# Expert stage of a two-layer graph network: one register load of TensorE moved behind the transposes, and the order of copies, scaling and adds on VectorE and GpSimd changed

## The reference

```
x = x + gnn0(layernorm(x), adj)          # (A @ (x @ W + b)) / column sums of A
x = x + ffn(layernorm(x))                # the expert stage, below
x = x + gnn1(layernorm(x), A)            # relu(D^-1/2 (A + I) D^-1/2 x @ W.T + b)
x = x + bit_operation(layernorm(x))      # adds 0 or 2 to columns 128..159

def ffn(x):                              # 8 experts, two for each row
    scores = softmax(x @ Wg + bg)
    the two best of 8, their scores divided by their sum -> combine[row, expert]
    h = gelu(x @ W1[e] + b1[e])          # 256 -> 1024
    y = h @ W2[e] + b2[e]                # 1024 -> 256
    return sum over e of combine[:, e] * y[e]
```

## Time and profile before

| what | value |
|---|---|
| median of 3 runs | 1072.77 us (1072.39 to 1073.36) |
| profiled execution, its time | 1071.65 us |
| its span in the profile | 1069.8 us |
| TensorE busy | 950.6 us, 89% |
| VectorE busy | 552.7 us, 52% |
| ScalarE busy | 402.5 us, 38% |
| GpSimd busy | 352.5 us, 33% |
| granted TensorE clock, mean over the span | 0.954 |

### The profile page before, as it was taken

How to read it: one execution, slowest core, us unless ns; L and a number is a source line. 1 busy time by engine, 2 the same in 40 slices (tenths; PEclk the granted TensorE clock), 3 DMA queues, 4 the chain that set the end, 5 groups by cost and what they waited for, 6 DMA issues and landing times. The chain is left out here.

```text
span 1069.8 us, 21961 instructions
## 1 busy us (share of the span) xinstructions
PE 950.6 (89%) x6628; PEld 613.0 (57%) x6629; DVE 552.7 (52%) x1631; ACT 402.5 (38%) x820; POOL 352.5 (33%) x414
## 2 busy tenths in 40 slices
PE   4988999999912799999999999999829999999993
PEld 1444544444411688888888888888714454444541
DVE  6744213137598655655556556566536334161654
ACT  4863659676787323232232332323202101010111
POOL 3510000024566234545445445454535320110110
PEclk9999999999965899999999999999969999999997
DMA  9886898899787422222323223233259978876770
GB/s 335 321 302 195 281 328 321 314 337 381 263 266 197 151 40 43 51 45 46 54 40 55 45 45 52 42 50 50 44 154 391 409 275 283 312 239 192 232 266 26
DMA packets 91023, 199.83 MB, mean 187 GB/s; under 512 B 13312, under 2 KB 46848, under 8 KB 90848
## 3 DMA queue, kind: packets, MB, share of 16 engines
q1 hardware_dynamic: 69248, 164.17, 43.8%
q0 software_dynamic: 17552, 30.88, 14.6%
q10 hardware_dynamic: 4176, 4.19, 1.2%
HBM read 176.54 MB, written 22.68 MB: 186 GB/s over the span
## 5 line engine op out<-in xcount | busy, mean ns | idle before, releaser
L956 PE MATMUL bank<-adj_f,feat 128*128 128x512 f16 x1024 | 239.2, 389 | 17.7 <-DMA adj_f<-in_adjT 16.0
L1217 ACT ACTIVATE act_f<-bank,b_sb 128x256 f32<-128x256 f32 x296 | 124.2, 471 | 288.5 <-PE bank L1157 288.5
L1157 PE MATMUL bank<-rT,experts 128*128 128x256 f16 x1776 | 202.3, 274 | 6.1 <-DVE rT L1240 2.2
L1169 PE MATMUL bank<-experts,act_h 128*128 x1776 | 203.1, 275 | 3.5 <-DVE y_f L1255 3.5
L1157 PEld LDWEIGHTS bank<-rT,experts 128*128 x1776 | 169.6, 98 | 38.7 <-issue 16.2
L1169 PEld LDWEIGHTS bank<-experts,act_h 128*128 128x128 f16 x1776 | 173.9, 99 | 24.5 <-issue 3.7
L1590 PE MATMUL bank<-adj_g,feat 128*128 128x512 f16 x768 | 178.5, 386 | 1.0 <-POOL feat L1420 1.0
L956 PEld LDWEIGHTS bank<-adj_f,feat 128*128 128x128 f16 x1024 | 97.2, 96 | 143.5 <-issue 15.3
L840 ACT ACTIVATE spent<-adj_f 128x1024 f16<-128x1024 f32 x128 | 135.1, 1055 | 33.7 <-DMA adj_f<-in_adjT 28.2
L1089 POOL DMA_INDIRECT x_rows<-y,token x74 | 119.2, 1611 | 68.5 <-DVE y L1265 49.0
L1590 PEld LDWEIGHTS bank<-adj_g,feat 128*128 128x128 f16 x768 | 73.6, 96 | 93.9 <-issue 1.5
(11 more groups left out here) (261 smaller groups left out, 889.4 us busy)
## 6 DMA issues: line engine op xcount, KB each, us to landing
adj_f<-in_adjT SPq DMA_DIRECT2D x128, 512.0 KB, 6.7
adj_g<-in_adjT SPq DMA_DIRECT2D x72, 512.0 KB, 6.9
adj_early<-in_adjT SPq DMA_DIRECT2D x24, 512.0 KB, 6.1
adj_g<-in_adjT SPq DMA_DIRECT2D x48, 256.0 KB, 3.1
unit_f<-in_W SPq DMA_DIRECT2D x16, 512.0 KB, 7.4
stage<-in_W SPq DMA_DIRECT2D x12, 512.0 KB, 6.2
x_ring<-in_x POOLq DMA_DIRECT2D x16, 256.0 KB, 6.9
x_rows<-agg SPq DMA_DIRECT2D x4, 1024.0 KB, 8.9
```

The costliest lines, as they stand in the source:

```text
L956: last = pe.matmul(mine(s)[ib * DC + c][:, :], feat0[:, j, h, c * P:(c + 1) * P], adj_0[j % RING][:, ib * HALF_SWEEP:(ib + 1) * HALF_SWEEP ...
L1157: last = pe.matmul(pb[2 + q][:, k * SLOT:(k + 1) * SLOT], w1_part(e * DC + (f // FQ * W2_UNIT0 + c), wh)[:, (f % FQ) * P:(f % FQ + 1) * P] ...
L1169: last = pe.matmul(pb[6 + r][:, 0:D], act_h[:, ah, f, r * P:(r + 1) * P], experts[:, ds(e * DC + (W2_UNIT0 + f // UH), 1), wh, (f % UH) * ...
L1217: last = a.activation(act_f[q][:, k, :], pb[2 + q][:, k * SLOT:(k + 1) * SLOT], ACT.Gelu, bias=b1_sb[:, ds(e * FC + (2 * q + k), 1)], scal ...
```

## The change

Five edits, all in the expert stage:

1. TensorE reads `e2` behind `transposes(s + 2)`, not at the top of the pass.
2. VectorE copies the shares (`gates`) before `rT`.
3. VectorE does `take_y(s)` ahead of the fourth `split_hidden`, not behind it.
4. GpSimd waits for each half of y by itself, add 0 for half 0 and add 1 for half 1, within the loop and after it.
5. `y_free` counts halves: GpSimd gives it after each add has landed (it begins at `SR`), and VectorE waits for it before each half that it scales.

```diff
         @block.gpsimd
-            pool.sem_inc(sem("y_free"), 1)
+            pool.sem_inc(sem("y_free"), SR)
...
-            def scaled(s):
-                pool.wait_ge(sem("y_scaled"), (s + 2) * SR)
+            def scaled(s, r):
+                pool.wait_ge(sem("y_scaled"), (s + 1) * SR + r + 1)
                 pool.sem_inc(sem("waited"), 1)
...
             with pool.Fori(0, last) as s:
-                scaled(s)
+                scaled(s, 0)
                 add_rows(0)
                 rows_free(s + 3)
                 gather(pool, token, AHEAD * SR)
                 landed_until(s, 0)
+                pool.sem_inc(sem("y_free"), 1)
+                scaled(s, 1)
                 add_rows(1)
                 pool.wait_ge(sem("rows_loaded"), (s + 5) * (16 * SR))
                 landed_until(s, 1)
                 pool.sem_inc(sem("y_free"), 1)
                 take_tokens(s + 1)
-            scaled(last)
             for r in range(SR):
+                scaled(last, r)
                 add_rows(r)
                 landed_until(last, r)
...
         @block.tensor
             with pe.Fori(0, last_slot) as s:
                 e = expert_of(s + 1)
-                e2 = expert_of(s)
                 pe.wait_ge(sem("rT_ready"), s + 2)
                 for q in range(FQ):
                     first_layer(s + 1, e, q)
                 transposes(s + 2)
+                e2 = expert_of(s)
                 second_layer_may_begin(s, e2)
...
         @block.vector
             def next_rows(s):
                 v.wait_ge(sem("rT_ps_ready"), s + 1)
-                v.tensor_copy(rT[...], pb[0][...]).then_inc(sem("rT_ready"), 1)
                 v.tensor_copy(gates[...], rows[...]).then_inc(sem("gates_taken"), 1)
+                v.tensor_copy(rT[...], pb[0][...]).then_inc(sem("rT_ready"), 1)
...
             def scale_y(s):
                 v.wait_ge(sem("y_taken"), s + 2)
                 v.wait_ge(sem("gates_taken"), s + 1)
-                v.wait_ge(sem("y_free"), s + 1)
                 for r in range(SR):
+                    v.wait_ge(sem("y_free"), s * SR + r + 1)
                     v.tensor_scalar(y[:, r, :], y_f[:, r, :], gates[...], None, ALU.mult).then_inc(sem("y_scaled"), 1)
...
             with v.Fori(0, last_slot) as s:
                 next_rows(s + 2)
-                for q in range(FQ):
+                for q in range(FQ - 1):
                     split_hidden(s + 1, q)
                 take_y(s)
+                split_hidden(s + 1, FQ - 1)
                 scale_y(s)
```

More of the change, by code:

```diff
@@ L1239, in next_rows @@
                 v.wait_ge(sem("rT_ps_ready"), s + 1)
-                v.tensor_copy(rT[:, :, :, :].rearrange("p h c n -> p (h c n)"), pb[0][:, :].bitcast(F16)).then_inc(sem("rT_ready"), 1)
                 v.tensor_copy(gates[:, ds(s * SR, SR)], rows[:, :, ds(D + e, 1)].rearrange("p r a -> p (r a)")
                               ).then_inc(sem("gates_taken"), 1)
+                v.tensor_copy(rT[:, :, :, :].rearrange("p h c n -> p (h c n)"), pb[0][:, :].bitcast(F16)).then_inc(sem("rT_ready"), 1)
             def split_late(k):
```

## The result

The changed kernel ran 1061.84 us in the median (1059.44 to 1062.92, 4 runs), the kernel before beside it 1072.58 (1071.67 to 1073.36, 4 runs): ratio 0.9897, 95% interval 0.9878 to 0.9916. That is 10.7 us less; forecast were 1063.3 us and a range of 1061 to 1067.5. The profiled execution took 1062.92 us with a span of 1061.1.

The account below looks back on a forecast made before the run. TensorE, busy 89% of the span, was taken as the bound, with a sequencer hole at each loop top. Terms -9.3 + 0.3 - 0.1 - 0.4 = -9.5 us gave 1063.3 us; range for 8 in 10, 1061 to 1067.5.

Parts of the forecast that it names:

- Where the hole is from: Top of the expert loop: TensorE's sequencer needs 2.2 us of control against 1.9 us of lead, leaving 0.266 us idle per slot.
- (a): Rival: the moved load is not covered behind the transposes, a new hole before each second layer, 1067 to 1070 us; chance 0.09.
- (b): Rival: the loop-top hole is a fixed restart after a branch, so moving a load changes nothing, 1072.4 us; chance 0.05.
- Part 1: Reading e2 behind the transposes takes 0.7 us off the loop top and closes the hole at 35 tops: -9.3 us.
- the bare load of the first pass: In loop pass 0 the transposes wait for gathered rows, so the moved expert load is not covered: +0.3 us (0 to 0.7).
- Part 2: Copying gates ahead of rT on VectorE: later rT +0.3, gather released sooner -0.45, sum -0.1 us, bounds -0.5 and +0.3.
- Part 3: Taking y ahead of the fourth split: last second layer starts some 1.5 us sooner but does not end the stage; worth 0.
- Part 4: Halves of y on GpSimd's chain of adds at the stage's end: net -0.4 us, bounds -1.0 and +0.6.
- GpSimd's cycle: In steady slots GpSimd's free cycle is 10.1 us against TensorE's 10.94, 0.8 us to spare, so it is not on the path.
- (c): Rival: GpSimd becomes the bound with a cycle of 11.3 us, gathers slip and transposes wait, total 1076 us; chance 0.04.
- The main term: The loop-top hole closed by moving the e2 load, 0.266 us at each of 35 loop tops: -9.3 us.
- (d): Case of more gain than forecast: prologue and end both at their good bounds, 1061.5 us or less; chance 0.04.

## Why the prediction was right, and where it was not

**Where the hole is from: right.** Control of 2.2 us against a lead of 1.9 was to give the hole. Adding a load to the top lengthened it by the load's price, taking one out closed it, and putting two at the new place opened one there of the size that lead and price give. Rivals (a), a leak at the new place, and (b), a hole that is no shortage of lead, both fell. The Trainium skill, "Advanced Engine Details and Errata", section Engine Queue Depths, gives TensorE a queue of 64 entries. The prediction's estimate of 3.5 us of lead, from these counted as pairs, does not hold for this program: with it the added load at the top (2.2 and 0.66 us of control) would have cost nothing, and it cost 0.66 us a slot.

**Part 1: right in size.** Forecast -9.3 us over 35 tops, and +0.3 for the bare load of the first pass, -9.0 together. The two periods differ by 0.279 us, for 35 tops -9.8; the bare load cost 0.55; edit 1 alone measured -8.9.

**Part 2: wrong, the largest miss.** Its sum was -0.1 us, bounds -0.5 and +0.3; edit 2 alone is -4.0, of which -3.8 lie in the prologue (the 0.5 at the end belong to part 4). The failed step is "released 0.6 sooner less the first 0.15, -0.45": it took the time from gather to landing as fixed. The prediction's own rows had the 2.87 us of waiting, but I read only who was waited for, not what else was in the DMA queues. In its place the runs show that the wait was the order of two issues, shown by holding SyncE's loads back without edit 2, and that the idle time also cost the clock: second layer 7.01 us, 5.40 without. A gather released 0.6 us sooner was worth some 4 us, since it came to lie ahead of 2 MB.

**Part 3: right** as far as it goes. The last second layer waits 1.80 us and not 3.5, 1.7 less where 1.5 was forecast, and does not end the stage. An effect in steady slots of 1 us or less is not excluded.

**Part 4: wrong in sign.** Forecast -0.4 us, bounds -1.0 and +0.6; the two traces of all five have +1.2 and +0.4 against before. Of its terms the earlier gather, -0.6, came: the end is 0.4 us shorter than before with edits 1 to 3 and 0.5 with edit 2 alone. What failed is the halves' own part, -0.4 and +0.5. Against edits 1 to 3 the halves made the end 0.8 us slower in one trace and 1.6 in the other, and the medians 3.5 and 3.4 us. The first step that failed is the gain of 0.4, that the two adds behind a token copy "need only the first half scaled". From copy to add it was 1.46 and 1.43 us, and is 1.50 and 1.38 in the changed kernel's first trace. The token copy itself, released together with VectorE's second scaling, takes 0.34 us there and 0.19 before. The other failed step is the next one, GpSimd's cycle.

**GpSimd's cycle of 10.1 us, with 0.8 to spare: too good.** Rival (c) did not happen, no transposes waited for rows in the loop, but the margin is nearly gone. After the late gather GpSimd runs free in the changed kernel:

```profile
675.32 1.58 POOL L1089 DMA_INDIRECT x_rows<-y,token  x1 [1.16 <-issue]
677.21 1.01 POOL L324 DMA_INDIRECT rows<-ln_rows,token  x1 [0.30 <-issue]
...
680.10 2.01 POOL L1089 DMA_INDIRECT x_rows<-y,token  x1 [0.60 <-issue]
684.62 0.34 POOL L1102 COPY token<-tokens 128x10 int32 x1 [2.50 <-DMA x_rows<-y,token]
...
688.02 1.01 POOL L324 DMA_INDIRECT rows<-ln_rows,token  x1 [0.30 <-issue]
```

Gather to gather, 677.21 to 688.02, is 10.8 us, and over the seven cycles from 677.21 to 753.63 the mean is 10.92, the period itself; the second add takes 2.01 us and not 1.61. So what it is late by stays until the end, some eight slots on, and lengthens it. With edits 1 to 3 the cycles from there on were 10.6 and 10.7 us in the mean (two traces) and it caught up, and so it did in the second trace of all five, with 10.7. That would give a kernel with two groups of times, and its nine runs do lie at 1057.9 to 1059.4 (three) and 1061.3 to 1062.9 (six); but only two of them have traces, so this link is argued and not shown.

**What is open:** why the halves cost 2 to 3 us in the median when the end accounts for 0.8 to 1.6, which of the two does it, and the stretch from last add to end, 282.4 to 284.1 us over these kernels with the same code.

The main term was right; that the whole came out so near the forecast was luck: two misses, -4 and about +2 to +3, had opposite signs. Without the halves' cost the time is 1058.3 or 1058.0 us, below the stated range of 1061 to 1067.5. Two sums in the prediction are slightly off as well: part 4's terms add up to -0.5 and not -0.4, and the good bounds of all parts together give 1062.0 us and not the 1061.8 of its range or the 1061.5 of (d). The best kernel measured is edits 1 to 3 (1058.3 and 1058.0), with edits 1 and 2 (1059.2), and edit 1 with SyncE's loads held back (1059.2), within the spread of it.

## What to carry to other kernels

A hole in TensorE that waits for nobody is to be sought in its sequencer's records: compare the lead it has at the loop's end with the control it does there, and move register loads to where matmuls are queued. Where an engine waits for a small transfer, look for large ones issued at the same moment by another queue before taking the time to landing as given. Splitting a wait in two adds semaphore work to the waiting engine; on a chain that this engine bounds, as at this stage's end, that work is paid (0.22 and 0.04 us here) and the earlier signal may bring nothing.

## What the runs showed of the hardware

- At a loop's end TensorE's sequencer was 1.8 to 1.9 us, some 18 matmuls with their weight loads, ahead of the array (575.1 to 576.9 before, 569.3 to 571.24 after). It did not run past a wait that was not yet met: with edit 1 alone the third transposes waited until 369.68 us and the expert load behind them began at 369.8. A register load cost it 0.66 to 0.7 us.
- A gather of 128 rows issued beside four loads of 512 KB landed 4.3 us after GpSimd had finished it (363.54 to 367.88). Issued 0.35 us ahead of them, it had landed within 2.5 us (366.37 to 368.87), and with the loads held back until it had landed, in 1.9 us (365.87 to 367.75).
- Every trace has a gather on GpSimd near the 28th slot that comes 1.1 to 1.5 us later than the period asks; it shows as "issue", and its cause is not in these traces.
- Behind the 2.87 us in which TensorE waited, the granted clock was 0.50 from 369 to 371 us, and 48 matmuls took 7.01 us; behind a wait of 0.42 us they took 5.41.
